# First stage of a routed language-model block: the next chunk's transposes, the key split, GpSimd's root and the row moments stand at other places

## The reference

```python
h = take(weight, token_ids)                      # 8192 x 256
x = (h - mean) / sqrt(var + eps)                 # layernorm
ct_q, ct_kv = x @ Wd_q + b, x @ Wd_kv + b        # latents, 128 columns
query = ct_q @ Wu_q + b + rope(ct_q @ Wq_r + b, cos, sin)
key   = ct_kv @ Wu_k + b + rope(x @ Wk_r + b, cos, sin)
value = ct_kv @ Wu_v + b
h = h + softmax(query @ key.T / scale) @ value @ Wo + bo    # 16 heads of 16
y = layernorm(h)
h = h + y + expert_of(y)                         # top-1 of 32 experts, capacity 320
```

## Time and profile before

| what | value |
|---|---|
| median of 3 runs | 3315.01 us (3313.55 to 3324.78) |
| profiled execution, its own time | 3315.87 us |
| profiled execution, span | 3314.0 us |
| PE busy | 3202.7 us (97%) |
| DVE busy | 2908.6 us (88%) |
| ACT busy | 2468.7 us (74%) |
| POOL busy | 565.3 us (17%) |
| first stage, to the end of the last full k | 0 to about 284 us |
| router stage | about 2916 to 3064 us |

### The profile page before, as it was taken

The page is one execution under the profiler, slowest core; times in us unless marked ns, Lnnn a source line. Parts: engine busy times, 40 slices in busy tenths (PEclk is TensorE's granted clock), DMA queues, the critical chain, the costliest instruction groups (busy, mean ns, idle before and its releaser), DMA issues.

```text
span 3314.0 us, 67613 instructions
## 1 busy us (share of the span) xinstructions
PE 3202.7 (97%) x27520; PEld 1369.7 (41%) x27520; DVE 2908.6 (88%) x3157; ACT 2468.7 (74%) x4578; POOL 565.3 (17%) x752
## 2 busy tenths in 40 slices
PE   7997999999999999999999999999999999986999
PEld 3443333333333333333333333333333333365666
DVE  6889999999999999999999999999999999567222
ACT  3331888888888888888888888888888888943221
POOL 7882000000000000000000000000000000046233
PEclk9997999999999999999999999999999999998999
DMA  6895213131313131313131313122222220168773
GB/s 201 256 299 159 54 49 72 37 72 37 72 38 72 38 74 38 72 40 72 37 72 39 83 34 79 39 70 44 65 45 58 45 83 21 37 204 305 231 238 101
DMA packets 269155, 305.40 MB, mean 92 GB/s; under 512 B 45270, under 2 KB 198399, under 8 KB 265517
## 3 DMA queue, kind: packets, MB, share of 16 engines
q1 hardware_dynamic: 256812, 271.63, 29.7%
q0 software_dynamic: 12032, 29.45, 2.7%
HBM read 165.81 MB, written 139.23 MB: 92 GB/s over the span
## 4 chain that ended last, share of the span: by engine, by line
PE 81%; ACT 4%; DVE 3%; issue 2%; POOL 1%; DMA 0%; another core or an unknown queue 0%; SPq 0%; POOLq 0%; DVEq 0%
PE ps_o L916 33%; PE ps_s L899 26%; PE ps_m L868 13%; ACT probs L1012 2%; PE ps_g L1592 2%; PE ps_y L1603 2%; PE ps_u L1592 2%; DVE max_parts L1027 2%; ACT weighted L992 1%; PE ps_td L1581 1%; ACT rows_c L1343 1%; POOL slot_rows L1257 0%; PE ps_s L883 0%; POOL shift_c L1234 0%; DVE stats_c L1377 0%
## 5 line engine op out<-in xcount | busy, mean ns | idle before, releaser
L1027 DVE TENSOR_REDUCE max_parts<-ps_m 128x2 f32<-128x1024 f32 x2048 | 2486.1, 1223 | 79.9 <-PE ps_m L868 71.5
L1012 ACT ACTIVATE probs<-ps_s 128x512 f32<-128x512 f32 x4096 | 2217.5, 597 | 312.3 <-PE ps_s L899 127.8
L868 PE MATMUL ps_m<-keys,queries 48*128 48x512 f32 x4096 | 1483.5, 453 | 17.1 <-DVE max_parts L1027 16.7
L899 PE MATMUL ps_s<-queries,keys 51*128 51x512 f32 x4096 | 1480.5, 447 | 9.5 <-ACT probs L1012 3.1
L916 PE MATMUL ps_o<-probs,vals 128*32 128x256 f32 x16384 | 1295.5, 391 | 0.0
L899 PEld LDWEIGHTS ps_s<-queries,keys 51*128 51x128 f32 x4096 | 610.5, 185 | 832.2 <-issue 785.2
L868 PEld LDWEIGHTS ps_m<-keys,queries 48*128 48x128 f32 x4096 | 595.4, 187 | 77.4 <-DVE max_parts L1027 50.2
L916 PEld LDWEIGHTS ps_o<-probs,vals 128*32 128x32 f32 x16384 | 329.4, 108 | 720.4 <-issue 699.0
L824 POOL TENSOR_TENSOR heads_out<-weighted,recip_rows 128x512 f32<-128x512 f32 x63 | 80.9, 1285 | 2147.4 <-DMA recip_rows<-recip_rows_dram 2147.4
L1663 DVE TENSOR_TENSOR hidden<-ps_u,silu 128x320 f32<-128x320 f32 x64 | 31.5, 492 | 127.4 <-PE ps_u L1592 101.6
L1639 ACT ACTIVATE silu<-ps_g 128x320 f32<-128x320 f32 x64 | 28.0, 438 | 134.1 <-PE ps_g L1592 82.8
(11 more groups left out here) (108 smaller groups left out, 1600.0 us busy)
## 6 DMA issues: line engine op xcount, KB each, us to landing
slot_rows<-empty SPq DMA_DIRECT2D x16, 1290.0 KB, 5.2
vext<-val SPq DMA_DIRECT2D x64, 256.0 KB
halves_q<-parts SPq DMA_DIRECT2D x64, 256.0 KB
halves_k<-parts SPq DMA_DIRECT2D x64, 256.0 KB
keys<-halves_k SPq DMA_DIRECT2D x32, 512.0 KB, 7.5
queries<-halves_q SPq DMA_DIRECT2D x128, 128.0 KB, 3.2
vals<-vext SPq DMA_DIRECT2D x32, 512.0 KB, 5.6
recip_rows<-recip_rows_dram SPq DMA_DIRECT2D x64, 256.0 KB
```

The lines of the kernel that those rows point to most:

```text
L868: mm = pe.matmul(ps_m[m % 2][:, h, :], queries_r[par][rows, qt, p, t * P:(t + 1) * P], keys_r[par][rows, p, c * 512:(c + 1) * 512], start= ...
L899: pe.matmul(ps_s[bank][:], keys_r[par][rows, p, k * P:(k + 1) * P], queries_r[par][rows, qt, p, :], start=True, stop=True).then_inc(scores ...
L1012: act.activation(probs[:, n % RING, :], ps_s[bank][:], ACT.Exp, scale=SCALE).then_inc(probs_ok[bank], 1)
L1027: dve.tensor_reduce(max_parts[:, lu % 2, :, p, t, c], ps_m[m % 2][:], AX.X, ALU.max).then_inc(maxima_ok[m % 2], 1)
```

## The change

In the first stage, four things move. TensorE's transposes of the next chunk stand between the rotary and the content part of the query (but in chunk 0). ScalarE's split of a chunk's keys stands in the next chunk, behind the copy of the transposed rows. GpSimd's `root` stands in front of both low parts, not between them. VectorE's moments stand right behind the statistics, ahead of the key's terms. Besides, var + eps and minus the mean are made by VectorE, by two `tensor_scalar` (`root_inputs`), and no longer by two `tensor_tensor` of GpSimd. In the router stage the same two instructions go to VectorE, behind the gate, and the moments go ahead of the gate.

```diff
             def root(b, k):
 
-                pool.wait_ge(stats_ok, after(b, k, CT))
-                pool.tensor_tensor(var_eps[:, k, :], mv[:, k, :, 1], eps_sb[:], ALU.add).then_inc(eps_ok, 1)
-                pool.tensor_tensor(neg_mean[:, k, :], no_mean[:], mv[:, k, :, 0], ALU.subtract).then_inc(neg_mean_ok, 1)
                 pool.wait_ge(eps_ok, after(b, k))
                 pool.tensor_tensor(rstd[:, k, :], var_eps[:, k, :], neg_half[:], ALU.pow).then_inc(rstd_ok, 1)
                 pool.wait_ge(rstd_ok, after(b, k))
-                pool.wait_ge(neg_mean_ok, after(b, k))
                 pool.tensor_tensor(shift[:, k, :], neg_mean[:, k, :], rstd[:, k, :], ALU.mult).then_inc(shift_ok, 1)
 
...
                 pool.tensor_tensor(sums[:, 0, 1, :], terms[:, 0, 2, :], terms[:, 0, 3, :], ALU.add).then_inc(sums_ok[0], 1)
                 if ahead:
                     gather(*ahead)
+                if not (last and k + 2 >= CPB):
+                    root(*((b, k + 2) if k + 2 < CPB else (b + 1, k + 2 - CPB)))
                 for x in range(2):
-                    if x == 1 and not (last and k + 2 >= CPB):
-                        root(*((b, k + 2) if k + 2 < CPB else (b + 1, k + 2 - CPB)))
-
                     pool.wait_ge(high_ok[x], after(b, k))
                     pool.tensor_tensor(parts[:, k % 2, x, 1].bitcast(F32R), full[:, x], parts[:, k % 2, x, 0], ALU.subtract).then_inc(low_ok[x], 1)
...
                 rotary(b, k, 0)
+                early = more and (b, k) != (0, 0)
+                if early:
+                    transpose(*nxt)
                 content(b, k, 0)
                 values(b, k)
-                if more:
+                if more and not early:
                     transpose(*nxt)
                 rotary(b, k, 1)
...
                 if more:
                     copy_nt(*nxt)
+                if (b, k) != (0, 0):
+                    split(*((b, k - 1) if k else (b - 1, CPB - 1)), 1)
                 split(b, k, 0)
                 if more:
                     copy_lat(*nxt)
-                split(b, k, 1)
                 if not (last and k + 2 >= CPB):
                     normalise(*((b, k + 2) if k + 2 < CPB else (b + 1, k + 2 - CPB)))
 
...
+            split(BATCH - 1, CPB - 1, 1)
...
+
+            def root_inputs(b, k):
+                dve.wait_ge(stats_ok, after(b, k, CT))
+                dve.tensor_scalar(neg_mean[:, k, :], mv[:, k, :, 0], -1.0, None, ALU.mult)
+                dve.tensor_scalar(var_eps[:, k, :], mv[:, k, :, 1], EPS, None, ALU.add).then_inc(eps_ok, 1)
 
...
                 if ahead:
                     row_stats(*ahead)
                     dve.wait_ge(stats_raw, after(*ahead, CT))
+                    row_moments(*ahead)
+                    root_inputs(*ahead)
                 rope_terms(b, k, 1)
-                if ahead:
-                    row_moments(*ahead)
                 dve.wait_ge(terms_ok[1], after(b, k, 4))
                 dve.tensor_tensor(sums[:, 1, 0, :], terms[:, 1, 0, :], terms[:, 1, 1, :], ALU.subtract).then_inc(sums_ok[1], 1)
                 dve.tensor_tensor(sums[:, 1, 1, :], terms[:, 1, 2, :], terms[:, 1, 3, :], ALU.add).then_inc(sums_ok[1], 1)
...
@@ -1465,9 +1461,11 @@
                     residual(*n)
                     row_stats(*n)
                     dve.wait_ge(stats_raw, after(*n, CT))
+                if more:
+                    row_moments(*n)
                 gate(b, k)
                 if more:
-                    row_moments(*n)
+                    root_inputs(*n)
                 counts(b, k)
                 own(b, k)
                 slots(b, k)
```

More of the change, by code:

```diff
@@ L368, in root @@
                 pool.wait_ge(rstd_ok, after(b, k))
-                pool.wait_ge(neg_mean_ok, after(b, k))
                 pool.tensor_tensor(shift[:, k, :], neg_mean[:, k, :], rstd[:, k, :], ALU.mult).then_inc(shift_ok, 1)
             pool.memset(neg_half[:], -0.5).then_inc(half_set, 1)
-            pool.memset(eps_sb[:], EPS).then_inc(half_set, 1)
-            pool.memset(no_mean[:], 0.0).then_inc(half_set, 1)
-            pool.wait_ge(half_set, 3)
+            pool.wait_ge(half_set, 1)
             for k in range(2):
@@ L569, in _ @@
             dve.memset(val[:], 1.0).then_inc(ones_set, 1)
-            row_stats(0, 0)
-            dve.wait_ge(stats_raw, CT)
-            row_moments(0, 0)
-            row_stats(0, 1)
-            dve.wait_ge(stats_raw, 2 * CT)
-            row_moments(0, 1)
+            for k in range(2):
+                row_stats(0, k)
+                dve.wait_ge(stats_raw, (k + 1) * CT)
+                row_moments(0, k)
+                root_inputs(0, k)
             dve.wait_ge(const_in, 16 * NCONST)
@@ L1108, in phase_c @@
         w_o, w_router, expert_no = router.w_o, router.w_router, router.expert_no
-        neg_half, eps_sb, no_mean, carry = router.neg_half, router.eps_sb, router.no_mean, router.carry
+        neg_half, carry = router.neg_half, router.carry
         token_no, att_t, emb = router.token_no, router.att_t, router.emb
@@ L1226, in root @@
             def root(b, k):
-                pool.wait_ge(stats_ok, after(b, k, CT))
-                pool.tensor_tensor(var_eps[:, k % 2, :], mv[:, k % 2, :, 1], eps_sb[:], ALU.add).then_inc(eps_ok, 1)
-                pool.tensor_tensor(neg_mean[:, k % 2, :], no_mean[:], mv[:, k % 2, :, 0], ALU.subtract).then_inc(neg_mean_ok, 1)
                 pool.wait_ge(eps_ok, after(b, k))
@@ L1381, in row_moments, with root_inputs @@
                     dve.bn_aggr(mv[:, k % 2, t, :], stats[:, t, :]).then_inc(stats_ok, 1)
+            def root_inputs(b, k):
+                dve.wait_ge(stats_ok, after(b, k, CT))
+                dve.tensor_scalar(neg_mean[:, k % 2, :], mv[:, k % 2, :, 0], -1.0, None, ALU.mult)
+                dve.tensor_scalar(var_eps[:, k % 2, :], mv[:, k % 2, :, 1], EPS, None, ALU.add).then_inc(eps_ok, 1)
             def base(b, k):
```

11 lines of the change are left out of this document (1 added, 10 removed).

## The result

The changed kernel takes 3326.73 us in the median (3324.65 to 3330.68), the kernel before 3314.28 beside it (3311.21 to 3324.78). The ratio is 1.0035, with a 95% interval of 1.0022 to 1.0047: slower, by less than 0.5%. The profiled execution has a span of 3322.9 us, against 3314.0.

A forecast was written before the change was run, and what follows sets the result against it. The prediction took GpSimd's loop, 16.01 us per chunk, to bound the first stage, with TensorE not the limit. Terms 15.0 + 0.4 - 0.2 + 0.8 = +16.0 on 3315.01 gave 3331.0, range 3319 to 3337.

The forecast's parts named there:

- The root in the loop: First stage, GpSimd: power and shift between gathers and low q add 1.29 us to the loop of 16.01.
- the term +15.0: First stage: twelve intervals with gathers, each 1.25 us longer (interval 17.25).
- Who comes first: First stage: L598 asks at 121.77, low q at 121.82; if L598 is first the loop is 17.25, otherwise 17.30.
- The rival in which VectorE keeps the lock for both sums: First stage: both sums pass ahead of low q, the second loop (16.44) sets the pace; +6.3, 3321; chance 0.14.
- My last rival: First stage: not slower, TensorE sets the pace, all chunks at 14.66; 17 less, 3298; chance 0.04.
- The lock rival: First stage: VectorE keeps the lock for both sums, L598 and L599, ahead of low q; 3321; chance 0.14.
- Store and ends: First stage: interval with the store's wait (19.54 before) 0, last two intervals +0.4, start of the program -0.2.
- The clock rival: First stage: TensorE's clock falls in each chunk, 0.15 to 0.5 per interval, +2 to +6; 3333 to 3337; chance 0.09.
- The router stage: VectorE's row longer by 2.8 to 5.6, waits for exponentials 3.3 less; +0.8 taken, bounds -3.3 and +5.6.
- The port rival: Router stage: the two `tensor_scalar` wait for a whole GpSimd instruction, 14 chunks, +14; 3345; chance 0.04.
- The sum: Whole kernel: 15.0 + 0.4 - 0.2 + 0.8 = +16.0 on the median 3315.01, giving 3331.0.

The follow-up runs named there:

- both: Changed kernel with transposes and key split at their old places, and GpSimd's low q waiting for VectorE's two sums k: 3305.03 us, ratio 0.9967.
- the order back: Changed kernel with the next chunk's transposes and the key split at their old places, root still in front: 3332.84 us, ratio 1.0046.
- the run with the root's inputs on GpSimd: Changed kernel with transposes and key split at their old places and root's two inputs made by GpSimd, no wait added: 3308.8 us, ratio 0.9974.
- the first stage alone: First stage of the changed kernel with the router stage of the kernel before: 3328.27 us, ratio 1.0048.
- the early transposes alone: First stage of the kernel before with only the transposes moved early, router stage of the changed kernel: 3350.67 us, ratio 1.0102.
- root back: Changed kernel with the root alone put back between low q and low k: 3365.37 us, ratio 1.0168.
- router edit alone: Kernel before with only the changed router stage (root inputs on VectorE, moments ahead of the gate): 3316.09 us, ratio 0.9997.
- key split ahead of the copy: Changed kernel with low q waiting for the sums k, and ScalarE's key split ahead of the copy of transposes: 3303.07 us, ratio 0.9961.

## Why the prediction was right, and where its sizes were off

**The root in the loop.** Shown. The power and the shift stand directly behind the gathers and cost 1.14 + 0.15, the 1.29 forecast. Predicted interval 17.25, measured 17.09 where steady and 17.18 in the mean of the twelve; the term +15.0 measured +14.3 (12 x 1.19, against 15.99 before). What I put too long is the step from low q to full k, 3.57 against a measured 3.44.

**Who comes first.** L595 came 0.10 ahead of low q where I had 0.05, in a steady chunk, and the three instructions ran in the order forecast: first sum 0.69, low q, second sum 2.84 (forecast 2.9). That this order costs what it should is shown from two sides, by a wait (interval 16.43, then 14.95) and by later arrival without a wait (14.67). The rival in which VectorE keeps the lock for both sums gave 16.44 as the next limit; the run that brought it about measured 16.43, and its time of 3319.8 stands 1.2 below that rival's 3321.

**What I missed in the reading** is that the root in the loop costs 1.29 only while low q stands locked between the sums. In "both" the root is still in GpSimd's row and the interval is 14.95, 1.0 below that of the kernel before. So the root made GpSimd's row longer, but the lock tied that row to full k, and this tie was already there in the earlier trace rows. I had priced the lock as part of the 3.62 and didn't ask what the loop would be without it. My last rival, TensorE's pace of 14.66, I judged by the gathers alone; with the order back it was 0.6 us of arrival away, as the run with the root's inputs on GpSimd shows. The lock rival took it as a question of who keeps the lock, and the runs show it as one of arrival: asked 0.6 later, both sums pass ahead of low q. I had worked out the two arrivals by sums of small terms, and that they stayed 0.1 apart is partly luck.

**Store and ends.** The interval with the store's wait took 19.12 against 19.54 before (forecast 0, measured -0.4); the last two intervals up to the last full k +0.3 (forecast +0.4); the start -0.4 (forecast -0.2). First stage in all: forecast +15.2, measured +13.8.

**TensorE.** It waits 1.61 us ahead of content q and 0.30 ahead of the transposes, 1.9 together, where I forecast about 2 in one piece. The clock rival did not occur in each chunk: in the first stage, from 26 us on, the granted clock is at 0.50 for two stretches of 3.4 us, from 185.9 and from 220.0, and otherwise at 1.00. The interval behind each of them is 17.51 instead of 17.1 (the first stage alone had one such stretch, at 185.2, and one such interval behind it), so a fall cost 0.4, within the 0.15 to 0.5 that I had estimated. With the early transposes alone it came in six intervals and cost 1.7 each.

**The router stage** is the term that was mis-sized: +0.8 forecast, -3.8 measured in the trace, just outside my lower bound of -3.3. I had counted one wait of VectorE in each of seven chunks, 3.3 us in all. The waits fall by 6.1 (11.4 to 5.3), as those ahead of `places` went too. I can't say that they are an effect of their own: with the router of before in the changed kernel there were none either, and the exponentials were waited for in every chunk instead, to about the same sum. The two `tensor_scalar` cost less than the 2.8 that I had put as the least: VectorE's busy time in the stretch is 2.1 longer, with medians of 0.139 and 0.161 for the two, each overlapping the next instruction. From -6.1 and +2.1, that is -4.0, short gaps make the -3.8.

The port rival fell: the longest of L546, among the gathers and the low parts of the first stage, is 0.422 (the median is 0.170), and 0.195 for its like in the router stage. The rule of the Trainium skill, SBUF — State Buffer, section Who interferes with whom, lets such an instruction wait for a whole one of GpSimd's; no run here shows that: a gather lasts about 1.0, a low part 2.36.

In the time itself the router edit can't be made out. Alone it gave a ratio of 0.9997, and taken out of the changed kernel 1.5 us in the median (0.2 if each is set against its own runs of before), against 2.4 to 3.8 in the traces. The twelve profiles with it have 115.6 to 120.6 for the stretch, the two without it 119.3 and 120.7. The three longest of the twelve (118.8, 118.9 and 120.6) hold another 3.4 to 10.2 us at half clock, ahead of the fall at the stretch's end that all 14 have, and neither of the two has such a one; the other nine have 115.6 to 117.6. So it does shorten the stretch where the clock holds. How much of that reaches the time stays open, between nothing and 4 us.

**The sum.** The forecast of 3331.0 is 4.3 above the measured 3326.73. Of the 16.0, the first stage gave 1.4 less and the router stage 4.6 less. The trace's account gives +8.9, with -1.1 between the stages that I had at nothing, and the medians +12.4. The gap between the two lies in which executions were profiled. Part of the forecast's closeness in the time is luck: by the trace's account it is 7 too high.

## What to carry to other kernels

Where two engines lock each other out, look who asks first in each chunk, and by how much: here an instruction that arrived 0.1 us after the first of two that stood back to back pushed the second back by its whole length. A wait that cost its engine 1.3 us of idling was worth 2.1 us per chunk (17.10 to 14.95, with the order back), since the next engine in the loop was the one served.

A move can be free only beside another. The early transposes were harmless with the root in front and cost 35 us without it, and the early key split cost 5.5 us per chunk without the early transposes. Undo them one by one before you call one of them good.

When a loop gets faster, look at the queues next: here it was 7 us of waiting for a store behind loads that nobody needed yet.

## What the runs showed of the hardware that was not expected

Behind the first stage TensorE's granted clock is 0.50 (1.2 of 2.4 GHz) for a stretch whose length varies. Busy time in windows, of the changed kernel (PE first, then PEld, DVE, ACT, POOL, and the granted clock third from the end):

```profile
320.00:340.00 20.00, 14.08 (x37) 5.00 (x35) 19.96 (x19) 0.27 (x1) 0.88 (x4) 0.50 0.02 4
340.00:360.00 20.00, 19.80 (x132) 9.59 (x132) 18.21 (x17) 14.39 (x27) 0.00 (x0) 0.76 0.11 29
```

and of the kernel with the root's inputs on GpSimd, whose first stage ended 27.0 us earlier:

```profile
320.00:340.00 20.00, 20.00 (x117) 6.95 (x116) 12.81 (x12) 9.51 (x18) 0.00 (x0) 0.50 0.00 1
340.00:360.00 20.00, 20.00 (x116) 7.16 (x112) 12.68 (x12) 9.55 (x18) 0.00 (x0) 0.50 0.00 1
360.00:380.00 20.00, 20.00 (x113) 6.66 (x109) 11.18 (x11) 9.64 (x19) 0.88 (x4) 0.50 0.48 81
```

In the first the clock is at half while TensorE is busy 14 of 20 us and VectorE all of them, so VectorE sets the pace. In the second it stays at half up to 380, with TensorE busy in all of the 60 us and VectorE 11 to 13 of 20: here TensorE sets the pace, at half speed. From the last full k to the first `top` that execution took 2678.3 us, the changed kernel's 2646.2. That is 32 us, most of what lies between the 3297.77 and the 3334.07 that were measured for this kernel. The profiled execution was the slowest of its seven; its mean granted clock was 0.974, that of the six others 0.983 to 0.986.

In all 14 profiles the two grow together:

| stretch at 0.50 behind the first stage | last full k to first `top` | profiles |
|---|---|---|
| 51.2 to 54.6 us | 2646.2 to 2652.7 us | 10 |
| 75.1 us | 2655.3 and 2658.8 us | 2 (root back, router edit alone) |
| 95.6 us | 2666.9 us | 1 (key split ahead of the copy) |
| 116.1 us | 2678.3 us | 1 (root's inputs on GpSimd) |

So in these kernels a single profile's span can be off by 30 us for a reason that lies in no edit, and an interval read within a stage is worth more than a span. Why the clock comes back sooner in one execution than in another was not tested.

The other surprises are small. Two `tensor_scalar` on 128x4 start 0.07 us apart while each lasts 0.17 to 0.35. A power on 128x4 on GpSimd takes 1.05 us. From the starts and durations I read that the waiting engine got its turn at the end of the instruction that it met, although the other engine had the next one ready 0.61 us after the last: behind the first sum in the changed kernel, behind the second where it asked 0.6 later.
